# Expert pipeline of an adaLN, attention and mixture-of-experts block: handoffs one round apart, eight result buffers, scatters released in two pairs

## The reference, cut to what matters

```python
logits = x @ gate_weight.T
probs = softmax(logits)
routing_weights, selected_experts = lax.top_k(probs, 8)
routing_weights = routing_weights / routing_weights.sum(-1, keepdims=True)
# per expert, with its weight column we (zero where the expert is not selected):
gate, up = jnp.split(x @ wgu, 2, axis=-1)      # 256 -> 2 x 96
act = silu(gate) * up
final = final + we[:, None] * (act @ wd)       # 96 -> 256
```

## Time and profile before

| | us |
|---|---|
| median of 3 runs | 521.24 (520.41 to 523.81) |
| span of the profiled execution | 576.6 |
| PE busy in it | 477.4 (83%) |
| DVE busy | 342.7 (59%) |
| ACT busy | 305.9 (53%) |
| POOL busy | 212.3 (37%) |

### The profile page before, as it was taken

One profiled execution on the slowest core, in us unless ns is written; L12 is line 12 of the kernel. 1 busy time (PEld: TensorE's weight loads), 2 busy tenths in 40 slices (PEclk: granted clock), 3 DMA queues, 4 the chain that ended last, 5 costly groups with the idle time before them and its releaser, 6 DMA issues. The chain is left out here.

```text
span 576.6 us, 10371 instructions
## 1 busy us (share of the span) xinstructions
PE 477.4 (83%) x3073; PEld 351.1 (61%) x3073; DVE 342.7 (59%) x1204; ACT 305.9 (53%) x854; POOL 212.3 (37%) x224
## 2 busy tenths in 40 slices
PE   4586999999899899999983766987988888888666
PEld 1366767877787678788653423765665666655322
DVE  4768496596685894795793564544355454553033
ACT  3456787885966887779864201333244343444200
POOL 0344110041114631025584642245444455445600
PEclk9799999999999999999996788999899899899879
DMA  8920862000301102002998739884444444330097
GB/s 283 411 70 19 167 131 74 1 1 0 76 1 54 69 30 73 2 1 74 345 404 291 278 107 298 227 288 129 111 115 115 113 128 127 107 95 13 19 363 304
DMA packets 47318, 79.49 MB, mean 138 GB/s; under 512 B 8266, under 2 KB 31127, under 8 KB 46880
## 3 DMA queue, kind: packets, MB, share of 16 engines
q1 hardware_dynamic: 36864, 55.34, 31.1%
q0 software_dynamic: 7680, 16.93, 8.2%
q10 hardware_dynamic: 2720, 6.55, 3.5%
HBM read 56.54 MB, written 26.44 MB: 144 GB/s over the span
## 5 line engine op out<-in xcount | busy, mean ns | idle before, releaser
L620 POOL DMA_INDIRECT pair_rows<-eout,dest x93 | 91.8, 987 | 99.5 <-ACT eout L634 78.2
L833 ACT ACTIVATE sact<-ps 128x192 f32<-128x192 f32 (+1 forms) x50 | 16.3, 325 | 122.7 <-remote 73.6
L1323 DVE SCALAR_TENSOR_TENSOR aact<-sact,wcol,ps 128x96 f32<-128x96 f32 x96 | 26.0, 311 | 92.6 <-issue 87.1
L1685 PE MATMUL ps<-wts,xg 128*64 (+1 forms) x512 | 71.5, 342 | 3.7 <-DVE copy_gu L1346 2.2
L691 ACT ACTIVATE lg<-lg,mneg 128x128 f32<-128x128 f32 (+1 forms) x128 | 56.4, 443 | 26.1 <-DVE mneg L1029 21.5
L1685 PEld LDWEIGHTS ps<-wts,xg 128*64 128x64 f32 x512 | 53.0, 143 | 16.5 <-issue 9.5
L541 POOL DMA_INDIRECT slot_rows<-rows,pair_slot x48 | 47.9, 998 | 37.2 <-issue 24.1
L1512 PE MATMUL ps<-oT,wo_sb 128*128 128x256 f32 x240 | 54.4, 380 | 0.0
L1706 PE MATMUL ps<-wts,aT 96*64 96x256 f32 (+1 forms) x256 | 49.8, 395 | 4.4 <-issue 3.4
L1512 PEld LDWEIGHTS ps<-oT,wo_sb 128*128 128x128 f32 x240 | 44.6, 190 | 6.2 <-ACT oT L634 0.7
L634 ACT ACTIVATE lg<-lg,rinv 128x128 f32<-128x128 f32 (+1 forms) x128 | 45.9, 448 | 2.5 <-issue 1.7
(11 more groups left out here) (237 smaller groups left out, 1184.4 us busy)
## 6 DMA issues: line engine op xcount, KB each, us to landing
wts<-in_experts_dram SPq DMA_DIRECT2D x22, 640.0 KB, 8.0
xrow<-slot_rows SPq DMA_DIRECT2D x192, 65.0 KB
pairs<-pair_rows SPq DMA_DIRECT2D x16, 512.0 KB, 11.2
wts<-in_experts_dram ACTq DMA_DIRECT2D x10, 640.0 KB, 6.1
slot_rows<-zero SPq DMA_DIRECT2D x1, 4160.0 KB, 24.2
wT<-in_wq_t_dram SPq DMA_DIRECT2D x4, 512.0 KB, 6.5
wq_raw<-in_wq_l_dram SPq DMA_DIRECT2D x1, 2048.0 KB, 14.6
wo_sb<-in_wo_l_dram SPq DMA_DIRECT2D x1, 2048.0 KB, 20.5
```

The costliest lines, as they stand in the source:

```text
L620: nc.gpsimd.indirect_dma_start(out=pair_d, out_offset=bass.IndirectOffsetOnAxis(ap=dest[:, d:d + 1], axis=0), in_=out_rows(d), in_offset=N ...
L1685: ins = nc.tensor.matmul(ps[h * R:(h + 1) * R, 2 + u % 2, k * I2:(k + 1) * I2], xg[u % len(xg)][:, k, cc, h * R:(h + 1) * R], moving, star ...
```

## The change

Nothing is computed otherwise. The instructions of a round are the same; their order on PE, ACT and DVE, their buffers and their waits change.

- PE's loop runs one round longer. In round g it alternates transposes of a group of g and `gate_up` of a group of g-1, then `turn_act` of g-2, then `down` of g-3.
- `gate_up` uses three banks (5, 2, 3) from group 8 on; both groups' turned activations share bank 4, so `turn_act` of a round waits until ACT has copied those of the round before, and `copy_turned` waits for both groups' transposes.
- ACT in round g: `silu` of g-1 (two buffers `sact`), `copy_turned` of g-2, `copy_down` of g-2, `copy_out` of g-3.
- DVE in round g, per group: copy of turned rows, `copy_gate_up`, then `weigh` of g-1; `find_rows` of both groups last.
- Results have eight buffers for six, as four pairs.
- POOL: the first scatter of round r, for r from 4 to 22, also waits until `down` of round r+1 is done, its third until `gate_up` of the first group of round r+4 is done.

```diff
     PER = NE // LOADS
-    NOUT = 6
+    NOUT = 8
     NPAIR = NT * TOPK
...
         o = 16 * KIB
-        xg = [at(f"xg{i}", [P, 2, CC, P], off) for i, off in enumerate((take(2 * KIB), take(2 * KIB), r3 + 10 * KIB, rows_off[0] + NOUT * KIB))]
+        xg = [at(f"xg{i}", [P, 2, CC, P], off) for i, off in enumerate((take(2 * KIB), take(2 * KIB), r3 + 10 * KIB, rows_off[0] + (NOUT - 2) * KIB))]
         wcol = at("wcol", [P, (NE + MORE) // 2], take(384))
-        sact = at("sact", [P, 2, I], take(2 * I * 4))
+        sact = [at(f"sact{i}", [P, 2, I], off) for i, off in enumerate((take(2 * I * 4), row_off + 2 * KIB))]
         aact0 = take(2 * I * 4)
...
         assert o <= spare + 5 * KIB
-        eout = at("eout", [P, NOUT, C], rows_off[0])
+        eout_pair = [at(f"eout{i}", [P, 2, C], off) for i, off in enumerate([rows_off[0] + 2 * i * KIB for i in range(NOUT // 2 - 1)] + [row_off])]
         eout_first = at("eout_first", [P, 3, C], r3 + 12 * KIB)
...
         NR = len(ROUNDS)
+        round_of = {g: r for r, gs in enumerate(ROUNDS) for g in gs}
         TABLE_AT = 5
...
         def out_rows(d):
-            return eout_first[:, d] if d < 3 else eout[:, d % NOUT]
+            return eout_first[:, d] if d < 3 else eout_pair[d % NOUT // 2][:, d % 2]
+
+        PLAIN = 8
+
+        def gu_bank(u):
+            return 2 + u % 2 if u < PLAIN else (5, 2, 3)[(u - PLAIN) % 3]
+
+        def gu_before(u):
+            return u - 2 if u < PLAIN else u - 3
+
+        PACED = range(TOPK // 2, NR - 4)
 
...
             for d in range(NDBL):
+                r = round_of[group_of[d]]
+                if r in PACED and d == GROUPS[ROUNDS[r][0]][0]:
+                    pool.wait_ge(dn_done, ROUNDS[r + 1][-1] + 1)
+                if r in PACED and d == GROUPS[ROUNDS[r][-1]][0]:
+                    pool.wait_ge(gu_done, ROUNDS[r + 4][0] + 1)
                 pool.wait_ge(out_copied, group_of[d] + 1)
...
                 n = len(GROUPS[a])
-                act.wait_ge(at_done, a + 1)
+                act.wait_ge(at_done, ROUNDS[round_of[a]][-1] + 1)
                 if a >= 2:
                     act.wait_ge(dn_done, a - 1)
-                copy(aT[a % 2][0:I, 0:n, :], ps[0:I, 4 + a % 2, 0:n * P].rearrange("p (k t) -> p k t", k=n)).then_inc(at_copied, 1)
+                copy(aT[a % 2][0:I, 0:n, :], ps[0:I, 4, a % 2 * 2 * P:(a % 2 * 2 + n) * P].rearrange("p (k t) -> p k t", k=n)).then_inc(at_copied, 1)
 
...
                 act.wait_ge(gu_done, u + 1)
-                if u >= 1:
-                    act.wait_ge(act_ready, u)
-                nc.scalar.activation(sact[:, 0:n, :], ps[:, 2 + u % 2, 0:n * I2].rearrange("p (k i) -> p k i", k=n)[:, :, 0:I],
+                if u >= 2:
+                    act.wait_ge(act_ready, u - 1)
+                nc.scalar.activation(sact[u % 2][:, 0:n, :], ps[:, gu_bank(u), 0:n * I2].rearrange("p (k i) -> p k i", k=n)[:, :, 0:I],
                                      ACT.Silu).then_inc(silu_done, 1)
...
                 else:
-                    copy(eout[:, d % NOUT:d % NOUT + n, :], ps[:, 6 + a % 2, 0:n * C].rearrange("p (k c) -> p k c", k=n)
+                    copy(eout_pair[d % NOUT // 2][:], ps[:, 6 + a % 2, 0:n * C].rearrange("p (k c) -> p k c", k=n)
                          ).then_inc(out_copied, 1)
...
             next_two = late_two
-            for g in range(NR + 2):
+            for g in range(NR + 3):
                 us = ROUNDS[g - 1] if 1 <= g <= NR else []
-                outs = ROUNDS[g - 2] if g >= 2 else []
-                for a in outs:
-                    copy_turned(a)
+                outs = ROUNDS[g - 2] if 2 <= g < NR + 2 else []
                 for u in us:
...
                 for a in outs:
+                    copy_turned(a)
+                for a in outs:
+                    copy_down(a)
+                for a in ROUNDS[g - 3] if g >= 3 else []:
                     copy_out(a)
-                for u in us:
-                    copy_down(u)
                 if g == 2:
...
                 for k, d in enumerate(GROUPS[u]):
-                    ins = V.scalar_tensor_tensor(out=aact[u % 2][:, k, :], in0=sact[:, k, :], scalar=wcol[:, d:d + 1],
-                                                 in1=ps[:, 2 + u % 2, k * I2 + I:(k + 1) * I2], op0=ALU.mult, op1=ALU.mult)
+                    ins = V.scalar_tensor_tensor(out=aact[u % 2][:, k, :], in0=sact[u % 2][:, k, :], scalar=wcol[:, d:d + 1],
+                                                 in1=ps[:, gu_bank(u), k * I2 + I:(k + 1) * I2], op0=ALU.mult, op1=ALU.mult)
                 ins.then_inc(act_ready, 1)
...
                 ins_ = ROUNDS[g] if g < NR else []
-                for x in ins_:
-                    copy_turned_rows(x)
-                    find_rows(x)
                 us = ROUNDS[g - 1] if g else []
                 for k in range(max(len(us), len(ins_))):
+                    if k < len(ins_):
+                        copy_turned_rows(ins_[k])
+                        copy_gate_up(ins_[k])
                     if k < len(us):
...
                         weigh(us[k])
-                    if k < len(ins_):
-                        copy_gate_up(ins_[k])
+                for x in ins_:
+                    find_rows(x)
                 if g == TABLE_AT:
...
                 pe.wait_ge(act_ready, a + 1)
-                if a >= 2:
-                    pe.wait_ge(at_copied, a - 1)
-                if a == TABLE_AT:
-                    pe.wait_ge(cols_read, 2)
+                if a == ROUNDS[round_of[a]][0] and a:
+                    pe.wait_ge(at_copied, a)
                 for k in range(len(GROUPS[a])):
-                    ins = T_(ps[0:I, 4 + a % 2, k * P:(k + 1) * P], aact[a % 2][:, k, :])
+                    ins = T_(ps[0:I, 4, (a % 2 * 2 + k) * P:(a % 2 * 2 + k + 1) * P], aact[a % 2][:, k, :])
                 ins.then_inc(at_done, 1)
...
                 pe.wait_ge(xt_copied, u + 1)
-                if u >= 2:
-                    pe.wait_ge(act_ready, u - 1)
+                if u == PLAIN:
+                    pe.wait_ge(cols_read, 2)
+                if gu_before(u) >= 0:
+                    pe.wait_ge(act_ready, gu_before(u) + 1)
                 for k, d in enumerate(GROUPS[u]):
...
                                 moving = copy_gu[m % NCOPY][:, cc * I2:(cc + 1) * I2]
-                            ins = nc.tensor.matmul(ps[h * R:(h + 1) * R, 2 + u % 2, k * I2:(k + 1) * I2],
+                            ins = nc.tensor.matmul(ps[h * R:(h + 1) * R, gu_bank(u), k * I2:(k + 1) * I2],
                                                    xg[u % len(xg)][:, k, cc, h * R:(h + 1) * R], moving, start=(cc == 0), stop=(cc == CC - 1))
...
 
-            for g in range(NR + 2):
-                outs = ROUNDS[g - 2] if g >= 2 else []
+            for g in range(NR + 3):
                 if g < len(IDLE):
                     keep_clock(IDLE[g])
-                for x in ROUNDS[g] if g < NR else []:
-                    turn_rows(x)
-                for a in outs:
+                xs = ROUNDS[g] if g < NR else []
+                us = ROUNDS[g - 1] if 1 <= g <= NR else []
+                for k in range(max(len(xs), len(us))):
+                    if k < len(xs):
+                        turn_rows(xs[k])
+                    if k < len(us):
+                        gate_up(us[k])
+                for a in ROUNDS[g - 2] if 2 <= g < NR + 2 else []:
                     turn_act(a)
-                for u in ROUNDS[g - 1] if 1 <= g <= NR else []:
-                    gate_up(u)
-                for a in outs:
+                for a in ROUNDS[g - 3] if g >= 3 else []:
                     down(a)
...
                     pe.wait_ge(cols_ready, 1)
-                    pe.wait_ge(at_copied, g - 1)
                     for k in range(3):
```

## The result

| | before | after |
|---|---|---|
| median of the runs, us | 521.4 (520.4 to 523.8) | 541.4 (540.1 to 542.0) |
| ratio, 95% interval | | 1.034 (1.027 to 1.040) |
| span of the profiled execution, us | 576.6; run again 522.3 | 539.5 |

The forecast was 529.5 us with a range up to 534. The direction is right, the size is not: the kernel is 20 us slower, and I had named 8.

A forecast was written before the change was run, and what follows sets the result against it. The prediction held PE to be already nearly full, at 5.8 to 6.2 us a round with handoffs hidden. From the 521.2 us median, 10.3 for the tail less 2 for the rounds gave 529.5 us, range 514 to 534.

The forecast's parts named there:

- the tail: From round 27's start to the pair loads: two rounds of scatters stand ahead, everything from the pair loads on 10.3 us later.
- the fill: Start of the expert stage: one down round moves from there into the dense part, which cancels any earlier round 27.
- the late signals: Dense rounds: PE's signals 2 to 4 us late, put down to recording; rival that they are real, about 512 us, chance 0.20.
- Order on PE: PE's rounds: no instruction more, waits already hidden; gain 0 to 0.4 us a round, 0.1 taken, 2 us in all.
- The gain that was to be had: Steady rounds: only what jitter breaks through 1.6 us of slack, 2 us in all.
- VectorE's order: VectorE's rounds: dest_ready at about 7.1 us instead of 1.9, delaying SP's row loads, hidden by 1.4 us.
- the slack that I named: Row loads in steady rounds: landed at 12.0 us, read at 13.4, so 1.4 us of cover.
- The third rival: VectorE, SP or POOL tie the rounds through late dest_ready or held-up copies: 7 us on top, about 536, chance 0.10.
- SP: SP's eight row loads a round: 4.3 us with register instructions, plus the gaps between them, fitting under PE.
- The second sact buffer, eight result buffers: ScalarE's SiLU waits of 0.72 us and eviction waits behind scatter landings: already hidden, so removing them gains nothing.
- the sign for this step: Tail: right if POOL keeps gaps of 0.30 without waiting for PE, pair loads some 20 us after round 27 begins.
- The rule on copies that lock GpSimd out of a shared port: VectorE copies beside POOL's scatters: next to no cost here; 0.08 us is the most a scatter has lost.

The follow-up runs named there:

- e9: Kernel before with one plain 128x128 fp32 product added between the two groups' gate-ups in each full round; median 533.5 us in a single run, regular round 6.51 us.
- e11: Kernel before with a pair of half-width 128x64 products added between the two gate-ups in each full round; median 525.0 us beside 524.9 for the kernel before.
- e4: Changed kernel with all of PE's transposes in one block a round, its other parts kept; 536.4 us, ratio 1.023.
- e0: Kernel before, unchanged, profiled a second time; ratio 0.9997, span 522.3 us.
- e1: Changed kernel without the pacing of the scatters; ratio 1.029, span 533.4 us.
- e8: Kernel before with one 128x128 transpose added between the two groups' gate-ups in each full round; median 534.1 us in a single run, regular round 6.35 us.
- e10: e4 with find_rows of each group right behind the copy of its turned rows on VectorE; 536.8 us, ratio 1.020.

## Why the prediction was right or wrong

The forecast was 11.9 us under the measured median, and the range ended 7 us below it. That the direction came out is owed to the tail, which held. By the forecast's own terms: the rounds were to give 2 us and cost 10.3, which is 12.3; the tail was to cost 10.3 and cost 10.8, 0.5; the fill was to cancel and gave 3.7, which takes that much off; and the profiled before (524.1 us as a run) stands 2.9 above the median that I started from. 12.3 + 0.5 - 3.7 + 2.9 = 12.0.

**What bounds the kernel, and the late signals: right.** I held the rounds to be at 5.8 to 6.2 us behind the 7.97 of the earlier trace rows; they are 5.94, mean 6.01. The kernel's span without the late signals gives 39.0 of the 54.3 us in the rounds, where I had reckoned 43. But I put the lateness to recording as such, and a second recording doesn't have it.

**Order on PE: the step that failed.** "Not an instruction more in a round" is true, and I took from it that the round can't get longer. I priced PE as so many steps of each kind, from rows inside a run of like instructions, and put the steps between one kind and the next at nothing. Those steps are what the change multiplies: they cost 0.30 us a block of transposes, and two blocks more a round make 0.59 us. The second execution of before shows most of the price in its timeline of PE, at its only block (and the last downs ahead of the next one):

```profile
419.55 1.09 PE L1387 MATMUL ps<-ident,xrow 128*128 128x128 f32 x8
420.47 0.60 PE L1387 MATMUL ps<-ident,aact 128*96 128x128 f32 x4
421.00 0.38 PE L1685 MATMUL ps<-wts,xg 128*64 x1
...
421.22 0.33 PE L1685 MATMUL ps<-wts,xg 128*64 x1
421.38 0.33 PE L1685 MATMUL ps<-wts,xg 128*64 x1
...
425.17 0.38 PE L1706 MATMUL ps<-wts,aT 96*64 x1
...
425.49 1.09 PE L1387 MATMUL ps<-ident,xrow 128*128 128x128 f32 x8
```

Eight row transposes go at (420.47 - 419.55)/8 = 0.115 us; the four behind them take 0.53 until the first product, 0.07 over four steps; that product takes 0.22 to the next where later ones take 0.16; and from the last pair of downs, 425.17 and 425.18, to the transposes behind it are 0.31 where a step of downs is 0.21. That makes 0.07 + 0.06 + 0.10 = 0.23, most of the 0.30. The assumption that a block costs only its instructions could have been tested before the result. The first trace has the same steps in its one round of 5.94 us, the first of the twenty (I had summed 5.8): eight row transposes in 0.93 us, and 0.52 for the four behind them.

```profile
371.43 1.09 PE L1387 MATMUL ps<-ident,xrow 128*128 128x128 f32 x8
372.36 0.60 PE L1387 MATMUL ps<-ident,aact 128*96 128x128 f32 x4
372.88 2.82 PE L1685 MATMUL ps<-wts,xg 128*64 128x192 f32 x32
```

In the round of the earlier trace rows the late signals fill the place between downs and transposes and hide it.

That full width against half width is the cause, and not transpose against product, is shown by e9 and e11. The Trainium skill has the rule for it (TensorEngine Tiling (Array Packing), section Tiling Modes, Key Properties): changing the tiling mode of the array drains it. The row transposes use 128 rows by 128 columns (those of the activations 96 columns), gate-up and down 128 or 96 rows by 64 columns; gate-up to down, same width, shows no gap (2.75 then 1.73 in one piece each). The runs agree with that rule, and put 0.30 us on a change there and back here. I had not weighed it.

**The gain that was to be had: nearly none, right.** PE had one round of 6.94 us with a wait of 0.93 for turned rows, and one of 6.40. After the change no round has a wait: 1.5 us saved in twenty rounds, 11.8 paid. How much of the saving is the decoupling's is only partly shown. e9, with the old lags and regular rounds of 6.51 us, still has one of 7.23, where the kernel after has none at 6.53; but with the blocks undone (e4) the new order has more long rounds than before, not fewer.

```profile
PE ps L1685 <- DVE xg L1306: 0.9, 1, 0.9
```

This is the line of e0's waits from 361 to 490 us; the kernel after has no such line there.

**VectorE's order: hidden in the change, not hidden by the slack that I named.** I gave 1.4 us of slack at rounds of 5.8. At 6.53 PE waits for nothing. Where the rounds are 5.94 (e4), PE does wait for rows that dest_ready released late; the loads took 6.8 us to land there and not the 2.6 that I borrowed from the scatter. The third rival had the right mechanism for another kernel. That its 536 us lies nearer to the measured 541.4 than my forecast is luck: nothing of what it named cost this kernel a wait on PE in the twenty rounds.

**SP: priced too low.** I gave it 4.3 us a round and the gaps between its instructions. In the second execution of before its 128 loads with run-time addresses are spread over 97.9 us, 6.2 us for the eight of a round, and SP waits for dest_ready once in all that time (the rows are those of line 429, and of SP's waits from 363 to 500 us):

```profile
L429 SPq FUSED_REGOPS  x128: 37/37/47, 365.2 to 463.1; - x128
SPq L429 <- DVE dest L1314: 0.2, 1, 0.2
```

That is more than PE's 6.01, so what hides it is the lead that ten buffers give. In e4 the chain of waits from 400 to 457 us is mostly SP: its row loads (L440) are 68.1% of it, its register loads (L469) 7.9%.

So a faster PE could have won little: the next limit seems to stand right beside it. No run tests this.

**The second sact buffer, eight result buffers: nothing, as said.** Neither ScalarE nor a landing is in the chain of waits over the twenty rounds.

**Tail: right.** Double 92's scatter was to start 20.9 us behind round 27's start and does so at 21.5; the pair loads follow 2.7 us on (said: 2.6). Before, 10.8 for the 10.6 said. POOL runs at gaps of 0.30 behind PE, as the sign for this step demanded. The split was not in the prediction: pacing 2.6 and the lag of a round 8.2 (e1).

**Fill: "which cancels it" was wrong** by some 3 us. The fill of the six executions with the downs a round later is 34.7 us in the mean (32.3 to 36.9), of the seven others 37.5 (35.2 to 40.2). 1.7 us of this are the downs moved behind round 7's start; the rounds counted from there have as many downs in both kernels, so nothing gives them back before the tail, where they are already counted. The ranges overlap, so the rest of the difference may be chance.

**The rule on copies that lock GpSimd out of a shared port** (the Trainium skill, SBUF — State Buffer, the "DVE blocks DMA" trap) would have moved scatters by what copies run beside them. The scatters' own time is 986 ns in the median after the change (93 of them, 984 to 1178) and 985 in the second execution of before (982 to 1025): the medians agree, and only the longest one is 0.15 us longer.

## What to carry to other kernels

On an engine that is full, price the boundaries and not only the instructions: read the step from the last of one kind to the first of the next beside the step inside a run, and multiply by how many boundaries a reordering makes. Here 0.30 us for a block of full-width transposes between half-width products, in 20 rounds with two blocks more, cost more than all the waits that the reordering could hide. When such a cost is taken away again, the next limit may keep most of the time (e4). And look at a second profiled execution before reasoning from waits that no instruction explains.

## What the runs showed of the hardware that was not expected

- A block of 128x128 instructions among 128x64 pairs costs PE 0.30 us beside its own time with transposes (5.94, 6.24, 6.53, 6.84 us for one to four blocks; e8 0.30), and 0.35 with an fp32 product (e9, against the same multiplications at half width), and nothing to be seen at equal width (e11: 0.22 us, the pair's own length in the chain). The granted clock was 1.00 in the rounds of both kernels.
- One profiled execution of the kernel before took 54 us longer than another, with PE's signals 2 to 4 us late for 20 rounds and at a clock of 0.97 there. None of the thirteen other profiled executions did; the cause is open.
- A row load of 65 KB took 6.8 to 7.4 us to land beside weight loads at the start of the steady part (e4, e10).
- SP needs 6.2 us for eight row loads with run-time addresses where each is 0.47 us by its own row: 97.9 us for 128 of them, nearly without a wait (e0).
